# Two-layer transformer kernel: second layer's query stacks transposed by DMA, later and smaller loads, two rounding products moved to ScalarE

## The reference

```
x = x + attention0(layernorm(x), ctx, mask per batch)      # Wq, Wk, Wv, Wo; softmax over 128 keys
x = x + ffn0(layernorm(x))                                 # 128 -> 512 -> 128
x = x + attention1(layernorm(x), ctx, one mask)            # the same 8x8 weights for every head
x = x + moe(layernorm(x))                                  # 8 experts 128 -> 256 -> 128, top 2

ffn0:  xq   = clip(round(x * 127/max|x|))     gate = silu(xq @ T(Wg)), up = xq @ T(Wu)
       hq   = clip(round(h * 127/max|h|))     h = gate * up;  out = hq @ T(Wd)
       # T rounds a weight to -1, 0 or 1 times the matrix's mean size; x and h are scaled back
moe :  y[e] = relu(x @ W1[e] + b1[e]) @ W2[e] + b2[e];  out = sum of the top two, weighted
```

## Time and profile before

| what | value |
| --- | --- |
| time, median of 3 runs | 214.71 us (214.35 to 215.3) |
| profiled execution's own time | 216.64 us |
| its span, first to last instruction | 214.8 us |
| PE busy | 196.6 us, 92% of the span |
| DVE busy | 162.4 us, 76% |
| ACT busy | 135.3 us, 63% |
| POOL busy | 82.7 us, 38% |
| DMA | 15.09 MB, mean 70 GB/s |

### The profile page before, as it was taken

How to read it: one execution, slowest core, us unless ns; L and a number is a source line. 1 busy time by engine, 2 the same in 40 slices (tenths; PEclk the granted TensorE clock), 3 DMA queues, 4 the chain that set the end, 5 groups by cost and what they waited for, 6 DMA issues and landing times.

```text
span 214.8 us, 6119 instructions
## 1 busy us (share of the span) xinstructions
PE 196.6 (92%) x2114; PEld 160.8 (75%) x2114; DVE 162.4 (76%) x608; ACT 135.3 (63%) x378; POOL 82.7 (38%) x197
## 2 busy tenths in 40 slices
PE   2487697999999999999999999999999999999992
PEld 0255474757766777777888988898979889999992
DVE  6458989999999999999987859966576736265225
ACT  3343466468868677766968579547955576566430
POOL 4494320432337544143520425438210604232532
PEclk9999889999999999999999999999999999999998
DMA  5849678504440724430080000400220000000000
GB/s 156 243 111 303 164 98 349 145 9 101 108 92 0 160 50 92 98 87 17 2 92 9 5 0 17 98 3 12 54 47 6 0 15 0 17 0 15 2 10 24
DMA packets 39747, 15.09 MB, mean 70 GB/s; under 512 B 34211, under 2 KB 38819, under 8 KB 39462
## 3 DMA queue, kind: packets, MB, share of 16 engines
q1 hardware_dynamic: 39142, 14.00, 27.7%
q10 hardware_dynamic: 576, 0.72, 1.0%
HBM read 5.80 MB, written 0.52 MB: 29 GB/s over the span
## 4 chain that ended last, share of the span: by engine, by line
PE 81%; DVE 7%; DMA 5%; issue 2%; SPq 2%; POOL 1%; ACT 1%; DVEq 0%; ACTq 0%
PE ps_B L826 14%; PE ps_A L839 12%; PE ps_O L756 7%; PE ps_B L690 7%; PE ps_A L675 6%; PE ps_B L692 6%; PE ps_Q L708 6%; PE ps_A L677 6%; DMA m0T_i<-in_mask0T 5%; PE ps_O L764 3%; PE ps_X L722 2%; PE ps_A L791 2%; PE ps_O L774 2%; PE ps_A L835 2%; PE ps_P L736 2%
## 5 line engine op out<-in xcount | busy, mean ns | idle before, releaser
L907 ACT ACTIVATE probs<-ps_B 128x512 f32<-128x512 f32 x64 | 36.5, 598 | 15.6 <-PE ps_B L692 14.8
L956 ACT ACTIVATE hid<-ps_B,b_sb 128x128 f32<-128x128 f32 x128 | 35.6, 378 | 15.3 <-PE ps_B L826 15.2
L1063 DVE TENSOR_REDUCE mx<-ps_A 128x4 f32<-128x512 f32 x64 | 42.0, 677 | 3.7 <-PE ps_A L677 3.7
L826 PE MATMUL ps_B<-mxT,w_sb 128*128 128x128 f32 x256 | 33.3, 278 | 0.0
L839 PEld LDWEIGHTS ps_A<-w_sb,hid 128*128 128x128 f32 x256 | 31.1, 192 | 0.6
L839 PE MATMUL ps_A<-w_sb,hid 128*128 128x128 f32 x256 | 31.2, 275 | 0.0
L826 PEld LDWEIGHTS ps_B<-mxT,w_sb 128*128 128x128 f32 x256 | 30.6, 192 | 0.5 <-issue 0.4
L654 POOL TENSOR_TENSOR yc<-yc 128x512 f32<-128x512 f32 (+2 forms) x21 | 17.3, 823 | 34.1 <-DVE yc L1228 33.0
L675 PE MATMUL ps_A<-m_b,id_b 128*128 128x512 bf16 x64 | 24.7, 385 | 2.4 <-DVE mx L1063 1.2
L692 PEld LDWEIGHTS ps_B<-qmT,kblk 118*128 118x128 bf16 x256 | 20.4, 100 | 8.6 <-issue 0.8
L692 PE MATMUL ps_B<-qmT,kblk 118*128 118x128 bf16 x256 | 25.5, 223 | 0.0
(11 more groups left out here) (135 smaller groups left out, 391.5 us busy)
## 6 DMA issues: line engine op xcount, KB each, us to landing
w_sb<-in_m1T SPq DMA_DIRECT2D x1, 1024.0 KB, 6.2
w_sb<-in_m2T SPq DMA_DIRECT2D x1, 1024.0 KB, 8.1
out_y<-out_sb SPq DMA_DIRECT2D x8, 64.0 KB, 1.5
x_sb<-in_x SPq DMA_DIRECT2D x1, 448.0 KB, 6.7
ctx_sb<-in_ctxT ACTq DMA_DIRECT2D x1, 448.0 KB, 5.5
m_i<-in_mask SPq DMA_DIRECT2D x1, 384.0 KB, 4.2
m0T_i<-in_mask0T SPq DMA_DIRECT2D x1, 384.0 KB, 5.0
kblk<-kst SPq DMA_TRANSPOSE x16, 3.7
```

Of the source, the lines that this page charges most:

```text
L826: mm = pe.matmul(psum("z", b, i)[:, c * P:(c + 1) * P], w1_sb[:, 4 * i + c, :], mxT[:, b % 2, :], start=True, stop=True)
L907: ends(act.activation(probs[:, n % 2, 4 * i:4 * i + 4, :], psum("exp", n, i)[:, :].rearrange("p (h k) -> p h k", h=4), ACT.Exp, scale=ATTN ...
L956: ins = act.activation(hid[:, b % 2, 4 * i + c, :], psum("z", b, i)[:, c * P:(c + 1) * P], ACT.Relu, bias=b1_sb[:, 4 * i + c:4 * i + c + 1])
L1063: ends(dve.tensor_reduce(mx[:, n % 2, 4 * i:4 * i + 4], psum("max", n, i)[:, :].rearrange("p (h k) -> p h k", h=4), AX.X, ALU.max), "dve.max")
```

## The change

The stacks of layer 1 (`pe.qs`, `act.qs`, `pe.qb`, `act.qb`, all for l = 1) are replaced by two DMA transposes of the whole stack from SyncE's queue, `sp.qs` and `sp.qb`. Layer 0 keeps its stacks on TensorE. The rings grow: `qst` from 3 to 4 buffers, `qT` and `qmT` from 2 to 3. `hr` and `xr` go from VectorE to ScalarE. The loads are cut into smaller pieces and spread over the first nine key transposes; the feed-forward weights `wf_sb` are loaded behind the fourth key block (n = 3) where they were behind the second. Two zeroings at the start leave VectorE's head: one is now on GpSimd, the other behind `dve.rk` of unit 0. Two pairs of tiles share memory. The planner has new durations, and `START` has six numbers for each unit where it had one. No matmul other than the transposes is added or removed: of TensorE's groups only L708 changes its count, from 256 to 128.

```
-UNIT_ORDER = ((0, 0), (0, 1), (0, 2), (0, 3), (0, 4), (0, 5), (1, 0), (1, 1), (0, 6), (0, 7), (1, 2),
+UNIT_ORDER = ((0, 0), (0, 1), (0, 2), (0, 3), (0, 4), (0, 5), (1, 0), (0, 6), (1, 1), (0, 7), (1, 2),
...
+QUERY_STACK = ((("pe.qs", 1, "pool.ql"), ("act.qs", 1, "pe.qs")),
+               (("sp.qs", 1, "pool.ql"),))
+SHIFTED_STACK = ((("pe.qb", 1, "dve.m3"), ("act.qb", 1, "pe.qb")),
+                 (("sp.qb", 1, "dve.m3"),))
-        ("dve.xr", 1, "dve.qi"),
+        ("act.xr", 1, "dve.qi"),
-        ("dve.hr", 1, "dve.h3"),
+        ("act.hr", 1, "dve.h3"),
...
+                if name == "qs":
+                    after(sp, "pool.ql", n)
+                    if n >= TSLOTS:
+                        after(sp, "pe.max", n - TSLOTS)
+                    if b >= 2:
+                        wait_landed(sp, b - 2, "qs")
+                    sp.dma_start_transpose(qT[:, n % TSLOTS, :, :], qst[:, n % QSLOTS, :, :].rearrange("p g c -> p (g c)")
+                                           ).then_inc(landed["qs"][b % 2], 16)
+                if name == "qb":
+                    after(sp, "dve.m3", n)
...
             def later_loads(n):

                 if n == 0:
+                    masks(1, 1, 2)
                     sp.dma_start(wo_sb[0][:, :], w0o).then_inc(s_wo, 16)
+                    sp.dma_start(x_sb[:, 4:NB, :], x[4:NB].rearrange("b t d -> t b d")).then_inc(s_x4, 16)
                 if n == 1:
-                    masks(1, 2, NB)
+                    masks(2, 2, 4)
+                    sp.dma_start(ctx_sb[:, 4:NB, :], ctxT[:, 4:NB, :]).then_inc(s_ctx4, 16)
+                if n == 2:
+                    masks(3, 4, NB)
+                if n == 3:
                     for k, src in enumerate((wg, wu, wd)):
                         sp.dma_start(wf_sb[:, k, :], src).then_inc(s_wf[k], 16)
-                if n == 2:
+                if n == 4:
...
-                if n == 3:
-                    sp.dma_start(w1_sb[:, :, :], m1T).then_inc(s_moe, 16)
-                    sp.dma_start(w2_sb[:, :, :], m2T).then_inc(s_moe, 16)
+                if n == 5:
...
+                if n in (5, 6, 7, 8):
+                    part = slice(4 * (n - 5), 4 * (n - 5) + 4)
+                    sp.dma_start(w1_sb[:, part, :], m1T[:, part, :]).then_inc(s_moe, 16)
+                    sp.dma_start(w2_sb[:, part, :], m2T[:, part, :]).then_inc(s_moe, 16)
...
+                if name == "hr":
+                    after(act, "dve.h3", b)
+                    if b >= 1:
+                        after(act, "dve.hq", b - 1)
+                    ends(act.activation(hr[:, :], z2[:, b % 2, :], ACT.Copy, bias=ROUND, scale=fs[:, b, 11:12]), "act.hr")
...
-            zeros(kst[:, 1, :, :, :]).then_inc(kst_zero, 1)
-            dve.memset(banks["O"][0][:, :], 0.0).then_inc(bank_zero, 1)
             def late_constants():
+                pool.memset(ones[:, :], 1.0).then_inc(ones_ready, 1)
+                pool.memset(rows3[:, :], 0.0).then_inc(small_ready, 1)
```

More of the change, by code:

```diff
@@ L47 @@
 KSLOTS = 5
+QSLOTS = 4
+TSLOTS = 3
+MSLOTS = 3
+BY_DMA = (1,)
+MASK_PART = {0: 0, 1: 1, 2: 2, 4: 3}
 EPS = 1e-5
@@ L118 @@
     ("dve.fn", 1, "pool.fp"),
-)
+) for l in range(2)]
 STEPS = (
-    (("dve.mk", 1),) + ATTENTION + (
+    (("dve.mk", 1),) + ATTENTION[0] + (
         ("dve.q0", 1, "dve.fn"),
@@ L145 @@
     ),
[L146 removed]
+    (("pool.xb", 1),) + ATTENTION[1] + (
         ("pe.mxT", 1, "dve.fn"),
@@ L196 @@
[L196 to L207, removed]
@@ L231 @@
+AFTER_KEYS = {"dve.mk": ((1, 0), (2, 1), (4, 2)), "dve.st": ((4, 0),), "pe.kv": ((4, 1),), "dve.ws": ((0, 3),),
+              "pool.m1": ((0, 4),), "pool.xb": ((0, 4),), "dve.bp": ((0, 4),)}
 AFTER_LAYER0 = ("dve.st", "pool.xb")
-LATENCY = 0.1
+LATENCY = 0.04
 SAME = 0.03
 PATIENCE = 0.01
-START = (-52, -44, 20, 12, 22, 133, 38, 67, 117, 100, 152, 77, 98, 83, 149, 113)
-BIAS = (
[L237 to L258, removed]
-)
@@ L262, in steps_of @@
+LAYER_TIME = ({}, {})
+GROUP = {name: k for k, names in enumerate(STAGES) for name in names.split()}
 def steps_of(n):
@@ L661, in _, with query_stack_ready, shifted_stack_ready @@
         def _(pe):
+            def query_stack_ready(n):
+                if units[n][0] in BY_DMA:
+                    wait_landed(pe, units[n][1], "qs")
+                else:
+                    after(pe, "act.qs", units[n][1])
+            def shifted_stack_ready(n):
+                if units[n][0] in BY_DMA:
+                    wait_landed(pe, units[n][1], "qb")
+                else:
+                    after(pe, "act.qb", units[n][1])
             def maxima_scores(n, i):
                 l, b = units[n]
+                if n == 0 and i == 0:
+                    pe.wait_ge(id_ready, 1)
                 if i == 0:
-                    after(pe, "act.qs", n)
+                    query_stack_ready(n)
                     wait_landed(pe, n)
@@ L885, in _ @@
                     after(act, "pe.q", n)
-                    if n >= 3:
-                        after(act, "pe.qb", n - 3)
+                    if n >= QSLOTS and units[n - QSLOTS][0] in BY_DMA:
+                        wait_landed(act, units[n - QSLOTS][1], "qb")
+                    elif n >= QSLOTS:
+                        after(act, "pe.qb", units[n - QSLOTS][1])
                     elif n:
```

248 lines of the change are left out of this document (150 added, 98 removed), and 7 rows, old and new, of the table START.

## The result

The changed kernel takes 217.77 us (median of three runs, 216.55 to 219.6) against 214.65 us (214.35 to 215.3) before: ratio 1.014, 95% interval 1.010 to 1.019. It is **3.1 us slower**, and 12.8 us above the forecast of 205.0. Its profiled execution took 217.77 us, with a span of 216.0.

What follows compares the result with a forecast made beforehand. VectorE and the start were taken to bound the kernel up to M, TensorE's stream the rest. From the 214.8 us span: -5.0 behind M, -0.8 VectorE, -4.0 start, giving 205.0 us; forecast 202 to 208 (chance 0.59), range 200.0 to 210.5.

Steps and rivals of the forecast that it cites:

- The DMA transposes: 0, at worst 1 to 2 us in the first unit.: Layer 1's query stacks: other TensorE work covers the 5.0 us chain to the shifted scores, so no cost, at worst 1 to 2 us.
- M: Milestone: end of unit 9's last maxima, the fortieth group; read at 95.0 us before, forecast near 89 to 90.
- Rival C: Query transposes late behind key transposes in SyncE's queue, up to 0.6 us exposed in seven units: 209 to 213; chance 0.06.
- D: Rival: same queue mechanism, slower than before; landings of 5.8 us leave 2.4 us exposed eight times: 224; chance 0.05.
- landings in layer 1 exceed 5 us: Sign that the forecast is wrong: DMA query transposes of layer 1 landing later than 5 us after issue.
- M is set by the start and VectorE.: Up to M: VectorE's 77.9 us of steps plus 17.1 us idle or waiting set M; TensorE's stream sets the rest.
- The start: -4.0.: Up to M: maxima of units 2 and 3 come 3 to 9 us earlier; -4.0 us, between nothing and 7.6.
- Rival A: The start gives nothing, as the first maxima are not earlier: 209.0 us; chance 0.17.
- VectorE -0.8: Up to M: hr and xr leave VectorE, later units' steps fill in; its work falls from 77.9 to 77.1 us.
- ScalarE 0: Takes hr and xr (7.2 us), gives up copies (9.5): 0; risk of 4.8 us if VectorE waits for it.
- Behind M: -5.0: TensorE's work after M falls from 113.6 to 108.6 us, chiefly twelve fewer stacks at 0.45 us; small losses left unchanged.
- Weights behind the fourth block 0, experts' weights 0: Later-placed weight loads cost nothing: both sets land before their readers need them; 0 us each.

Runs made afterwards that it cites:

- experiments 1: Changed kernel without layer 1's 16 query transposes, TensorE reading both stacks from a static buffer: 213.89 us, ratio to before 0.9955.
- experiment 5: Changed kernel with one DMA issue moved, the shifted stack of unit (1,0) ahead of the key transpose of (0,7): 213.60 us, ratio to before 0.9947.
- experiment 9: Five runs with VectorE work cut or moved: four on experiment 5 (214.09 to 219.21 us), one on the kernel before (214.15 us).
- experiment 7: Experiment 5 with all loads as in the kernel before: 216.57 us; with the experts' weights together behind the sixth key transpose: 214.16 us.
- experiment 6: The kernel before, unchanged, profiled again: 214.46 us, span 212.6, mean clock 0.996.
- experiment 4: Changed kernel with the two rounding products back on VectorE, each right ahead of its reader: 221.51 us, ratio to before 1.029.
- experiment 8: Kernel before, own loads and order, with rounding on ScalarE: 217.88 us; with layer 1's stacks by DMA: 223.91 us; with both: 221.06 us.
- loads5: Experiment 5 with the experts' weights all behind the sixth key transpose: 214.16 us, ratio to before 0.9965.
- old_loads: Experiment 5 with all loads at the places and in the pieces of the kernel before: 216.57 us, ratio to before 1.0085.
- late_bp: Experiment 5 with the five VectorE steps that split the output bias moved behind M: 217.60 us, ratio to before 1.014.
- hoist_bp: As late_bp, with unit (0,4)'s query stack and maxima also moved forward, against experiment 5: 219.21 us, ratio to before 1.019.
- before_dma: Kernel before with layer 1's query stacks by DMA, orders kept, nothing else changed: 223.91 us, ratio to before 1.044.

## Why the prediction was wrong, step by step

- **"The DMA transposes: 0, at worst 1 to 2 us in the first unit."** Failed, and in the first unit. The cover there, counted as 3.8 us, was about that (5.0 with TensorE's own short waits), and 3.7 for a landing was not far off where nothing stands in the way (3.4 there, 2.7 as a rule). What I left out of this unit is SyncE's queue: 1.4 us until its turn (74.50 to 75.91), and then a landing of 4.3. With the half clock behind the pause it costs 3.9 us (experiments 1 and 5). Rival C's mechanism and place were right, at a chance of 0.06, but it was priced in seven units, not in the one with the least cover, and without what the pause does to the clock. D did not come: the second wait is only 0.9. The sign "landings in layer 1 exceed 5 us" did come once, a query stack of 5.8 us at 118 us, and nothing waited for it. The Trainium skill ("VectorE: DVE Perf Modes", section "The three transpose paths") puts one 128x128 tile by the DMA crossbar at 1309 ns, which an estimate would make 10.5 us for a stack of eight. The traces don't bear that out: most stacks of eight tiles land in 2.7 us, the slowest in 5.8.
- **"M is set by the start and VectorE."** Failed. VectorE's busy share does not make it the bound (experiment 9); before, the chain from 44 us up to M is TensorE's. The sum "steps by starts plus idle time" fitted M, and would have fitted it whatever the cause.
- **"The start: -4.0."** Failed against the kernel before. The key transposes went out as forecast (third at 16.05 forecast 16.4, fourth at 21.6 instead of 19.4), so the mechanism came, and in the new order the new loads do bring M 4.3 us forward (experiment 7). But units 2 and 3 are not M: against the kernel before the gain is gone at the fifth unit. The first maxima come 2 us later, where I forecast "not earlier"; TensorE's order there, which I did not look at, is where most of it lies (experiment 6). The upper bound of 7.6 took all 17.1 us as idle time to be won; 7.7 us of idle lie in the first 20 even at full clock, and from 20 to 90 only 1.0 of 70 is left. The windows from 20 to 80 us, which the earlier trace rows leave out, would have told it: even with the stretch of half clock VectorE is idle for 2.1 of the 70 us there. Rival A named this, at 0.17; its 209.0 still holds the 5.8 us of the other two terms.
- **"VectorE -0.8"** moved nothing by itself. Rounding on ScalarE gained 3.7 us (experiment 4), and **"ScalarE 0"** held in the new order. In the old one the risk that I priced at 4.8 us came in full (experiment 8).
- **"Behind M: -5.0"** (5.1 by its own terms). Right in sign, mis-sized: -2.5 measured. TensorE's last matmul ends 115.7 us behind M before and 113.2 in experiment 5, for 113.6 and 108.5 us of work by the prediction's prices: if the work is as counted, 2.6 us of the gain went back in small losses, 4.7 instead of 2.1. I had left these out as unchanged. What makes them larger stays open.
- **"Weights behind the fourth block 0, experts' weights 0"**: held (`loads5` 214.16, `old_loads` slower).
- **The base.** The profiled execution of before held 3.4 us of half clock at 25 us; at full clock, M is at 92.9, not 95.0, so 2 us of its M were never to be won. That the span of 214.8 could stand for the median time was luck: the stretch makes it some 2 us too long, and every execution's time is 1.8 us above its span.

By medians: a forecast of -9.7; measured +3.1. The query transposes, nearly all of it the one late stack, are 3.9 of the 12.8 between, shown. The other 8.9 are the start and M (M forecast 4.8 us earlier, found 1.1 later: 5.9) and the half of the gain behind M that did not come (2.5), which together are 8.4. Why the new order holds M where it is, and which order would pass on the early maxima, stays open: two attempts (`late_bp`, `hoist_bp`) made it worse.

## What to carry to other kernels

Before a step moves into a DMA queue, look at the one unit where the order leaves it least cover, and count what stands ahead of it in that queue at that time, issue included; put latency-critical issues ahead of those with slack. A busy engine is a bound only if the chain runs through it: where two engines are nearly always busy, cut a little work on one and see if the milestone moves before a sum rests on it. Parts and order go together: the same two parts gained 3.7 and 3.3 us in one order and lost 3.0 and 9.0 in another.

## What was not expected of the hardware

A DMA transpose of a key stack, 1.6 us to issue as a rule, took 3.51 us right behind two loads of 256 KB, and 2.90 at 16.05 us, right behind another one. The query stack issued after the first landed in 4.3 us instead of the 3.4 that it took in seven profiles with that stack issued first, with and without such loads near; once it took 4.6 there too. That the loads are the cause is not shown.

A pause of TensorE of 2.5 us was followed by 3.4 us of half clock, one of 1.4 at the same place in another execution by 3.4 too, and with a pause of 0.2 there was none. A long pause is not needed for it, nor does it always bring it: the kernel before has 3.4 us of half clock from 25 us on, with four waits of 0.5 to 0.9 us in the 7 us ahead and none longer, and `before_dma` none behind a wait of 1.9 at 90 us.
